# A graph network's edge gathers: index columns read in place, row slots freed one at a time

## What is computed

```python
h = relu(layernorm(x)); n = 6250
h = gcn_conv(h, src, dst, ones, W1, b1)            # pass 0: sum over edges of h[src]*norm, into dst
h = h / max(norm(h), 1e-12)
ev  = sigmoid(h[src] @ We1[:H] + h[dst] @ We1[H:] + be1)
na  = relu(segment_sum(ev[:, None] * h[src], dst) @ Wn1 + bn1)     # pass 1
ev2 = sigmoid(na[src] @ We2[:H] + na[dst] @ We2[H:] + be2)
g   = relu(segment_sum(ev2[:, None] * na[src], dst) @ Wn1 + bn1)   # pass 2
out = x + gcn_conv(g, src, dst, ev2, W2, b2)       # pass 3
```

## Time and profile before

| | |
|---|---|
| median of 3 runs | 6434.93 us (6432.22 to 6438.82) |
| span of the profiled execution | 6459.6 us |
| gathers (L441, POOL) | 3328, 948 ns each |
| pair products (L736, PE) | 7040 matmul records, 3520 pairs |
| POOL / DVE / PE / ACT busy share of the span | 51% / 37% / 41% / 14% |

### The profile page before, as it was taken

How to read it: one execution, slowest core, us unless ns; L and a number is a source line. 1 busy time by engine, 2 the same in 40 slices (tenths; PEclk the granted TensorE clock), 3 DMA queues, 4 the chain that set the end, 5 groups by cost and what they waited for, 6 DMA issues and landing times. The chain is left out here.

```text
span 6459.6 us, 78329 instructions
## 1 busy us (share of the span) xinstructions
PE 2679.0 (41%) x8018; PEld 1804.9 (28%) x8019; DVE 2411.2 (37%) x8424; ACT 903.4 (14%) x2361; POOL 3296.7 (51%) x3528
## 2 busy tenths in 40 slices
PE   1333333346444444344464444443345343433443
PEld 1322322334232222222242222222223233322332
DVE  4333333335333333333353333333344333333334
ACT  4000000003222222222231121211123000000000
POOL 6555555554544544444444544444443555555555
PEclk8555555557666666666676666666667555555555
DMA  3111111112222222222222222222222111111111
GB/s 95 40 38 40 40 37 40 40 41 69 75 67 66 69 64 66 71 66 66 59 88 64 70 62 66 69 63 65 66 65 81 45 37 38 40 36 39 39 40 52
DMA packets 236072, 366.86 MB, mean 57 GB/s; under 512 B 118303, under 2 KB 151923, under 8 KB 236020
## 3 DMA queue, kind: packets, MB, share of 16 engines
q0 software_dynamic: 134912, 332.75, 18.6%
q1 hardware_dynamic: 97522, 32.56, 2.1%
q10 hardware_dynamic: 3618, 1.35, 0.1%
HBM read 342.12 MB, written 23.49 MB: 57 GB/s over the span
## 5 line engine op out<-in xcount | busy, mean ns | idle before, releaser
L441 POOL DMA_INDIRECT rows<-table,idx_ring x3328 | 3153.6, 948 | 2978.3 <-SPq L348 1969.3
L736 PE MATMUL ps<-rows,weights 128*128 x7040 | 2493.5, 503 | 3630.1 <-issue 1516.5
L736 PEld LDWEIGHTS ps<-rows,weights 128*128 128x128 f32 x7040 | 1658.2, 283 | 4465.4 <-issue 4328.0
L1034 DVE TENSOR_TENSOR acc<-acc,ps 128x128 f32 (+2 forms) x3520 | 1251.1, 355 | 2546.2 <-issue 1750.2
L629 ACT ACTIVATE step<-xbuf,rows 128x128 f32 x1760 | 653.1, 400 | 2226.4 <-issue 1068.2
L1021 DVE SCALAR_TENSOR_TENSOR weights<-iota,pair_dst,step 128x128 f32<-128x128 f32 x880 | 305.4, 349 | 409.8 <-issue 351.9
L1018 DVE SCALAR_TENSOR_TENSOR weights<-iota,pair_dst,step 128x128 f32<-128x128 f32 x880 | 301.1, 348 | 399.4 <-issue 317.9
L1024 DVE TENSOR_SCALAR weights<-iota,pair_dst,gate 128x128 f32<-128x128 f32 x880 | 307.6, 361 | 271.5 <-issue 250.1
L1016 DVE TENSOR_SCALAR weights<-iota,pair_dst 128x128 f32<-128x128 f32 x880 | 256.0, 299 | 297.8 <-issue 268.2
L581 ACT ACTIVATE rows<-ps 128x128 f32<-128x128 f32 x49 | 13.6, 278 | 1403.5 <-PE ps L772 1402.9
L629 ACT ACT_TABLE_LOAD x55 | 70.6, 1283 | 356.6 <-issue 223.7
(11 more groups left out here) (134 smaller groups left out, 574.6 us busy)
## 6 DMA issues: line engine op xcount, KB each, us to landing
rows<-table,idx_ring POOLq DMA_INDIRECT x3328
table<-tab SPq DMA_DIRECT2D x12, 903.0 KB, 4.7
idx_ring<-edge_src SPq DMA_DIRECT2D x418, 4.0 KB
table<-acc SPq DMA_DIRECT2D x13, 448.0 KB, 3.0
out_nodes<-acc SPq DMA_DIRECT2D x6, 448.0 KB
table<-tab SPq DMA_DIRECT2D x2, 516.0 KB, 4.3
acc<-dst_s,lb_idx POOLq DMA_INDIRECT x49
table<-tab SPq DMA_DIRECT2D x2, 387.0 KB, 4.0
```

Source lines behind the costliest of these rows:

```text
L441: nc.gpsimd.indirect_dma_start(rows[:, u, 0:row_floats[k]], None, tables[k], bass.IndirectOffsetOnAxis(ap=idx_ring[:, u:u + 1], axis=0)).t ...
L736: nc.tensor.matmul(ps[u % W_RING][:, 0:WIDTH[k]], weights[:, u % W_RING, :], rows[:, bass.ds(slots[u], 1), 0:WIDTH[k]].rearrange("p o f -> ...
L1034: nc.vector.tensor_tensor(sums, sums, ps[u % W_RING][:, 0:WIDTH[k]], ALU.add).then_inc(pairs_added, 1)
```

## The change

The indices of all edge tiles stand in SBUF already, one column per tile, in `edge_src`. The change drops the ring of index columns with its staging DMAs and lets each gather read its own column of `edge_src`. [...] The two semaphores of the halves are replaced by one, `slots_free`. SP raises it after each tile: once tile *j* has landed and all pairs of tiles up to *j* - 6 are done. Gather *t* waits for *t* - 9 such raises in its pass, that is, until tile *t* - 10 has landed and tile *t* - 16 is done. The first 16 gathers of a pass wait for no slot. SP now loads 16 values at the head of a turn (L320 of the new file) in place of one for each half.

```diff
-HALF = UNROLL // 2
+LAG = 6
...
-        entry_row = sb("entry_row", [1, TABLE], i32)
+        entry_row = sb("entry_row", [1, LAG - 1 + TABLE], i32)
...
-        idx_ring = sb("idx_ring", [PART, UNROLL], u32)
...
-            def stage(turn, h):
-                sp.dma_start(idx_ring[:, h * HALF:(h + 1) * HALF],
-                             edge_src[:, bass.ds(turn * UNROLL + h * HALF, HALF)]).then_inc(idx_staged[h], 16)
...
             def relay_pass(k):
-                sp.wait_ge(entry_ready, 1)
+
                 with sp.Fori(0, GATHER_TURNS) as i:
-                    for h in range(2):
-                        _, (entered,) = nc.values_load_multi_w_load_instructions(
-                            entry_row[0:1, bass.ds(i * UNROLL + h * HALF, 1)], engines=[SYN], min_val=0, max_val=PAIRS,
-                            skip_runtime_bounds_check_because="entries are bounded when they are made")
-                        for u in range(h * HALF, (h + 1) * HALF):
-
-                            sp.wait_ge(landed[u], i * 16 + 16 * (GATHER_TURNS * k + 1))
-                            sp.sem_inc(tiles_landed, 1)
-                            if u == h * HALF + HALF // 2 - 1:
-
-
-                                sp.wait_ge(pairs_done, entered + (PAIRS * k + W_RING))
-                                sp.sem_inc(half_free, 1)
-                                sp.wait_ge(idx_staged[1 - h], i * 16 + 16 * (GATHER_TURNS * k + 1 + h))
-                                sp.sem_inc(half_ready[1 - h], 1)
-
-                        stage(i + 1, h)
-
+                    entered = nc.values_load_multi_w_load_instructions(
+                        entry_row[0:1, bass.ds(i * UNROLL, UNROLL)], engines=[SYN], min_val=0, max_val=PAIRS,
+                        skip_runtime_bounds_check_because="entries are bounded when they are made")[1]
+                    for u in range(UNROLL):
+
+                        sp.wait_ge(landed[u], i * 16 + 16 * (GATHER_TURNS * k + 1))
+                        sp.sem_inc(tiles_landed, 1)
+
+                        sp.wait_ge(pairs_done, entered[u] + (PAIRS * k + W_RING))
+                        sp.sem_inc(slots_free, 1)
...
                 pool.wait_ge(tab_stored[k], 16 * (NODE_TURNS if k == 0 else len(PIECES)))
-                with pool.Fori(0, GATHER_TURNS) as i:
-                    for h in range(2):
-
-                        pool.wait_ge(half_ready[h], i + (GATHER_TURNS * k + 1))
-                        pool.sem_inc(half_begun, 1)
-                        for u in range(h * HALF, (h + 1) * HALF):
-                            nc.gpsimd.indirect_dma_start(rows[:, u, 0:row_floats[k]], None, tables[k],
-                                                         bass.IndirectOffsetOnAxis(ap=idx_ring[:, u:u + 1], axis=0)).then_inc(landed[u], 16)
+                for t in range(GATHERED):
+                    if t >= UNROLL:
+
+                        pool.wait_ge(slots_free, GATHERED * k + t - UNROLL + LAG + 1)
+                    nc.gpsimd.indirect_dma_start(rows[:, t % UNROLL, 0:row_floats[k]], None, tables[k],
+                                                 bass.IndirectOffsetOnAxis(ap=edge_src[:, t:t + 1], axis=0)).then_inc(landed[t % UNROLL], 16)
...
-            act.activation(edge_src[:, GATHERED:GATHERED + UNROLL], ps[4][:, 0:UNROLL], ACT.Copy).then_inc(setup_moved, 1)
...
-            nc.vector.tensor_single_scalar(entry_row[:, :], first[1], float(PAIRS), ALU.min).then_inc(entry_ready, 1)
+            nc.vector.memset(entry_row[:, 0:LAG - 1], 0).then_inc(entry_ready, 1)
+            nc.vector.tensor_single_scalar(entry_row[:, LAG - 1:], first[1], float(PAIRS), ALU.min).then_inc(entry_ready, 1)
```

More of the change, by code:

```diff
@@ L31 @@
 PAIRS = TURNS * UNROLL
-BLOCKS = -(-max(PAIRS, GATHERED + UNROLL) // PART)
+BLOCKS = -(-max(PAIRS, GATHERED) // PART)
 TABLE = BLOCKS * PART
@@ L210, in gnn_kernel @@
             sem(n) for n in ("w1T_sent", "w1T_ready", "b1_rep_ready", "w_prod", "w_prod_ready"))
-        idx_staged, half_ready = ([sem(f"{n}{h}") for h in range(2)] for n in ("idx_staged", "half_ready"))
-        half_free, half_begun = sem("half_free"), sem("half_begun")
+        slots_free = sem("slots_free")
         landed, tiles_landed = [sem(f"landed{u}") for u in range(UNROLL)], sem("tiles_landed")
@@ L308, in _ @@
             sp.dma_start(pair_row[0:1, :, :], pair_rows[:, :]).then_inc(ld_pair_row, 16)
-            def stage(turn, h):
-                sp.dma_start(idx_ring[:, h * HALF:(h + 1) * HALF],
-                             edge_src[:, bass.ds(turn * UNROLL + h * HALF, HALF)]).then_inc(idx_staged[h], 16)
-            sp.wait_ge(setup_moved, 3)
-            for h in range(2):
-                stage(0, h)
-            sp.wait_ge(idx_staged[0], 16)
-            sp.sem_inc(half_ready[0], 1)
             def store(k, tab, lo, n):
@@ L331, in relay_pass @@
             def relay_pass(k):
-                sp.wait_ge(entry_ready, 1)
                 with sp.Fori(0, GATHER_TURNS) as i:
-                    for h in range(2):
-                        _, (entered,) = nc.values_load_multi_w_load_instructions(
-                            entry_row[0:1, bass.ds(i * UNROLL + h * HALF, 1)], engines=[SYN], min_val=0, max_val=PAIRS,
-                            skip_runtime_bounds_check_because="entries are bounded when they are made")
-                        for u in range(h * HALF, (h + 1) * HALF):
-                            sp.wait_ge(landed[u], i * 16 + 16 * (GATHER_TURNS * k + 1))
-                            sp.sem_inc(tiles_landed, 1)
-                            if u == h * HALF + HALF // 2 - 1:
-                                sp.wait_ge(pairs_done, entered + (PAIRS * k + W_RING))
-                                sp.sem_inc(half_free, 1)
-                                sp.wait_ge(idx_staged[1 - h], i * 16 + 16 * (GATHER_TURNS * k + 1 + h))
-                                sp.sem_inc(half_ready[1 - h], 1)
-                        stage(i + 1, h)
+                    entered = nc.values_load_multi_w_load_instructions(
[6 more added lines that the diff above has]
+                        sp.sem_inc(slots_free, 1)
+            sp.wait_ge(entry_ready, 2)
             for i in range(NODE_TURNS):
@@ L462, in scale_rows @@
                                         rnorm[:, t].unsqueeze(2).to_broadcast([PART, GROUP, HID]), ALU.mult).then_inc(pool_scaled, 1)
+            pool.wait_ge(setup_moved, 2)
             gather_pass(0)
@@ L705, in _ @@
             pe.wait_ge(ld_w, 16 * 13)
-            pe.wait_ge(setup_moved, 5)
+            pe.wait_ge(setup_moved, 4)
             for c in range(2):
@@ L994, in _ @@
             v.wait_ge(ld_pair_row, 16)
-            v.wait_ge(setup_moved, 5)
+            v.wait_ge(setup_moved, 4)
             nc.vector.memset(tab2[:, :, ONE:ONE + 1], 1.0)
```

## The result

The changed kernel took 5669.76 us (median of four runs, 5646.78 to 5670.31), the kernel before 6436.88 in the same set (6432.22 to 6471.27). The ratio is 0.8786, 95% interval 0.875 to 0.8821: 12% faster, where 4.7% was forecast, and outside the range. The profiled execution took 5646.78 us, its span is 5645.0 us, against 6459.6 before, so 815 us have to be found.

The account below looks back on a forecast made before the run. It took POOL's pauses, lengthened by starved engines and release by halves, as the bound. Savings of 307 us in passes 1 and 2 and under 10 in 0 and 3, together about 300, gave 6435 - 300 = 6135 us; range 5800 to 6490.

Parts of the forecast that it names:

- starved: State of DVE or SP under gathers: an instruction that otherwise takes 17 to 21 ns takes 0.7 us.
- The pause: POOL's stop between gathers, restarting after one tile: 4.8 us start to start, 3.55 over the 1.25 us cadence.
- good end: Shortest pause assumed for POOL: 2.35 us over the cadence, from the trace's pauses of 2.81 and 2.64 us idle.
- The work of a cycle: Tiles PE finishes per pause and burst: 7.65 in passes 1 and 2, 9.3 in pass 0, before the relay's deduction.
- The sum: Step times: 1.79 us in passes 1 and 2, 1.68 in passes 0 and 3; together about 300 us saved.
- SyncE's relay: SP's three in-order instructions per tile, some 4.2 us when starved: one tile off each cycle, ends none and two.
- my slower rival: SP's relay holds slots back, two or more tiles a cycle: 6515 us; chance 0.14.
- much faster: Short pauses throughout, 1.55 us a step in all passes: 930 us saved, 5505 us; chance 0.15 for below 5830.
- At nothing: Parts costed at zero: 418 staging DMAs removed, SP's longer register load, POOL's waits and jump, set-up changes.
- Straight-line code: POOL's 3328 unrolled gathers: cadence stays 1.25 us, with 1.41 us as the other end if POOL starves.
- POOL starves: POOL's unrolled gathers slow down, 530 us on the cadence less the 300: about 6670 us; chance 0.07.
- Nothing moves: POOL's pauses shorten and multiply in proportion: 6435 us, within 30 us or so; chance 0.14.

Follow-up runs that it names:

- j2: f2 with POOL also waiting, after every 4th gather, until that gather has landed; 5880.37 us, 0.910 of the kernel before.
- f3: f2 with POOL waiting for its slots eight at a time; 5668.78 us, 0.880 of the kernel before.
- f2: The changed kernel with the two tables that engines wait against held as 16-bit values; 5774.06 us, 0.897 of the kernel before.
- h2: f3 with SyncE testing pairs and freeing a half once per eight tiles, after the 6th landing, not testing at each landing; 6231.97 us, 0.981 of before.
- e4: e1 with the lag set to 2 in place of 6; 5403.36 us, 1.190 of the kernel before, on a chip that doesn't starve.
- f4: f2 with the index copies of eight columns put back in SyncE's queue, twice per turn, with their waits; 5877.54 us, 0.911 of before.
- e3: e1 with SyncE's two staging copies of eight index columns per turn put back; 4800.77 us, 1.057 of the kernel before.
- e1: The changed kernel with all three tables of wait numbers held as 16-bit values; 4764.75 us, 1.049 of before, on a chip that doesn't starve.
- h4: f3 with the loops of VectorE and TensorE in passes 0 and 3 holding 4 pairs instead of 16; 5905.59 us, 0.930 of before.
- e2: e1 with POOL waiting for slots eight at a time; 4928.76 us, 1.085 of the kernel before.
- set e: The runs e1 to e4, testing parts of the change on a chip that doesn't starve; the kernel before took 4542.74 us there.
- k1: f2 with POOL waiting, after every 6th gather, until that gather has landed; 5440.92 us, 1.197 of before, on a chip that doesn't starve.
- j1: f2 with POOL writing 256 floats per partition of a scratch buffer after every 4th gather; 5807.88 us, 0.899 of before.

## Why the prediction was wrong, point by point

*The direction and the bound.* Faster was right. That the passes are held by starved sequencers, and not by PE's or DVE's work, held on these chips: the long instructions are there before and after, and j2, which removes nearly all of them, runs its passes at POOL's own pace. That it is a chip's condition I could not know from one trace, and didn't consider. For my picture of a store of instructions that isn't refilled the runs give nothing: the instruction queues moved 20 packets in the whole of before.

*The mechanism.* "Finer release makes many short pauses of few long ones" is not where the gain came from. Put back to a grain of eight, the changed kernel is no slower (f3, 0.880 against f2's 0.897). The short pauses came with SyncE's test at each landing (h2, 0.981), which I had booked as a cost. So the direction was right in good part by luck.

*The pause: the step of the sum that failed.* I took 3.55 us over the cadence for each pause, because "each pause has a dead start" of 3.5 us from the last gather to the next add. That was read off a pause behind sixteen gathers in a row, where the engines had run dry. Behind short rows they haven't: that is my reading of the difference. The pauses themselves are measured. After has 568 gaps of more than 2 us between starts, together 970 us over the cadence: 1.71 us each (1.89 in passes 1 and 2, 1.46 in 0 and 3), half the term and below my good end of 2.35. Counted from 1.4 us up it is 886 gaps of 1.24 us. The good end was two pauses of 2.81 and 2.64 us, the shortest after which I saw the engines run freely. The trace of before had few shorter ones, as its pauses average 8.7 us over the cadence, and one stands in the same rows, 1.86 us. I treated them as the shortest possible.

*The work of a cycle.* The sum had 6.65 tiles for each pause in passes 1 and 2, and 8.3 in 0 and 3. By gaps over 2 us it was 5.1 and 6.8. That alone would have made the kernel slower than forecast; the pauses shrank by more. With the measured terms my formula gives 1.62 and 1.46 us a step (1.66 and 1.51 measured; the rest is in gaps under 2 us).

*SyncE's relay: wrong in sign.* I charged a tile per cycle for it, and my slower rival was built on it. The runs show its test as the source of the gain (h2 against f3). SyncE does go slowly, 2501 long instructions against 1527, and what that costs by itself wasn't measured; but testing at each landing keeps the halves apart and the rows short. That passing on may go too slowly is right all the same, in another place: a lag of 2 costs 13% on the chip that doesn't starve (e4).

*The sum.* Passes 1 and 2 took 1.63 and 1.68 us a step where I had 1.79, passes 0 and 3 both 1.51 where I had 1.68 and no gain at all. I had named passes 0 and 3 gaining as much as 1 and 2 as a sign that the loss was in the halves alone: they gained 9% and 11%, against 16% and 16%. The outcome is the rival *much faster*, 1.55 in all passes, to which I gave 0.15. Against before's median it lies at 5670, between its 5505 and its upper bound of 5830. The range, with 5800 below, left it out. (Half way from 6135 to 5505 is 5820, where I wrote 5800; it changes nothing.) That rival was worked out from short pauses by finer release, so its number came near and its cause did not.

*At nothing.* The staging wasn't nothing: 103 us on this chip (f4 against f2), 36 on the other (e3 against e1). I had looked only at what SyncE waited for, and not at what the copies add to a sequencer that is itself slow; that this is how they cost is likely, not shown. SyncE's load of 16 registers took 0.97 us, as costed.

*Straight-line code.* Right. 1.25 us between gathers and none of POOL's instructions long, so the rival *POOL starves* fell. The Trainium skill ("Runtime: NRT & Kernel Launch", Instruction fetch mechanics) has a sequencer stream unrolled code with the cost mostly hidden; the trace agrees. It also has a taken branch stall when its target lies outside a window of two blocks. Loops a quarter as long kept the long instructions (h4), on another chip the same loops had none (e1), and the instruction queues moved 20 packets in before and 45 in after, so such stalls don't explain these rows.

*Nothing moves* fell with the pauses: their number grew fivefold and their sum fell by a third.

## What to carry to other kernels

A relay that hands on arrivals is also a governor. When a ring is refilled by bursts, look at how many transfers go in a row and not only at how many slots are released at a time; on the starved chips, testing progress at every arrival kept the bursts apart, and releasing in small pieces brought nothing; on the other chip the small pieces were worth 3.4% (e2). A term read from the shortest pause in a trace is a bound for that kernel's pattern, not for the one that the change makes: give the range the pattern's own freedom. And time a kernel on more than one chip before its bound is explained, since one chip's condition can be worth 40%.

## What the runs showed of the hardware that was not expected

- The same kernel, the same inputs: 4541 to 4547 us in two sets, 6323 to 6471 in the three others and in the comparison with the change. The difference is in sequencer instructions: DVE's waiting instruction of the add at 21 ns always in the former; 0.7 us for one in seven of VectorE's register, branch and semaphore instructions (2529 of some 17900) in the latter, on every engine but POOL, while gathers follow each other at 1.25 us. The five sets ran on five chips (13 and 10 at 4543 us; 9, 0 and 12 at 6350 to 6465), so I put it down to the chip; no chip was met twice, the runs don't exclude another cause that lasted through a set, and what makes the instructions long isn't known. It doesn't follow TensorE's granted clock: in set e before took 4543.65 us at a mean of 0.648 and 4543.63 at 0.757. DMA was busy 14 to 30% of a pass, and the time in which a gather lands does not grow along a row: the median from its start to its last packet is 2.1 us in passes 0 and 3 of before and 2.4 in 1 and 2, at the 1st gather as at the 15th.
- The traces of the starved chips lack most of the records of landings. Each of the 3328 gathers raises its semaphore 16 times, 53,248 in all; before's trace holds 6212 of these, after's 10,599, e1's 52,812, k1's 53,231, and j2's, on a starved chip, 32,640. The times of all these runs come with a recorded span and clock, and no run shows how the kernels do when nothing is recorded. So that recording takes part in making the instructions long is a rival that stands untested.
- On a chip that does it, letting every 4th gather land before the next is issued (2.72 us from start to start) nearly removed it: 21 long instructions of VectorE in place of 2019, 405 of SyncE in place of 2345. Steps of 1.44 us with POOL at work did not (1989 and 2371).
- A load of 16 registers from a 16-bit table took 3.3 to 3.8 us by engine; on PE, in the same run, 3.79 us against 1.11 from a 32-bit table.
- A write of 256 floats per partition at POOL took 0.33 us and made the step between two gathers 0.19 us longer; 832 of them cost next to nothing while POOL waits anyway (j1 0.899, f2 0.897).
